# Two waits in GpSimd's scatter bursts of a routed expert kernel

## The reference

```python
x = x + _L0_attn_ref(_layernorm(x, axis=-1), ...)
x = x + _L0_ffn_ref(_layernorm(x, axis=-1), ...)
# within _L0_ffn_ref, N = 2048, TOP_K = 6, E = 64, C = 384:
topk_w, topk_idx = jax.lax.top_k(softmax(x @ gate_w.T), TOP_K)
pos = jnp.arange(A) - offsets[se]              # place of a token in its expert's list
buf = jnp.zeros((E, C, D)).at[se, pos_c].add(x[st])          # the scatter
eo = einsum(silu(einsum(buf, w_gate)) * einsum(buf, w_up), w_down)
y = jnp.zeros_like(x).at[st].add(eo[se, pos_c] * sw)
```

## Time and profile before

| what | us |
|---|---|
| median of 3 timed runs | 542.45 (541.57 to 545.41) |
| span of the profiled execution | 581.2 |
| start, 0 to 43 | 43.0 |
| attention and routing steps, 43 to 238.7 | 195.70 |
| tail of routing, 238.7 to 276.3 | 37.60 |
| loop over experts, 276.3 to 545 | 268.70 |
| closing, 545 to 581.2 | 36.2 |

### The profile page before, as it was taken

One profiled execution on the slowest core, in us unless ns is written; L12 is line 12 of the kernel. 1 busy time (PEld: TensorE's weight loads), 2 busy tenths in 40 slices (PEclk: granted clock), 3 DMA queues, 4 the chain that ended last, 5 costly groups with the idle time before them and its releaser, 6 DMA issues.

```text
span 581.2 us, 13626 instructions
## 1 busy us (share of the span) xinstructions
PE 528.9 (91%) x4267; PEld 446.2 (77%) x4267; DVE 348.5 (60%) x1107; ACT 301.3 (52%) x899; POOL 334.4 (58%) x365
## 2 busy tenths in 40 slices
PE   8799998988989894969999999999988999999991
PEld 7698988888889883858877878787766787778681
DVE  4968877777777874756554555555454555455512
ACT  3797777778777863311234444455544444445410
POOL 4482254555444546575146766766666676678840
PEclk9898998889777976899999999999999999999997
DMA  9999997722222222122999999999989999977556
GB/s 292 388 373 394 404 390 280 228 84 84 73 74 74 83 74 88 57 98 78 321 267 300 252 245 230 236 244 251 251 217 231 241 238 233 231 143 115 73 116 140
DMA packets 65857, 119.01 MB, mean 205 GB/s; under 512 B 11216, under 2 KB 43280, under 8 KB 62704
## 3 DMA queue, kind: packets, MB, share of 16 engines
q0 software_dynamic: 24576, 56.39, 37.0%
q1 hardware_dynamic: 39584, 58.75, 33.2%
q10 hardware_dynamic: 1616, 2.90, 1.4%
HBM read 57.28 MB, written 60.23 MB: 202 GB/s over the span
## 4 chain that ended last, share of the span: by engine, by line
PE 75%; DVE 7%; issue 4%; another core or an unknown queue 4%; ACT 4%; POOL 2%; DMA 1%; ACTq 0%; DVEq 0%
PE PS L958 17%; PE PS L976 9%; PE PS L962 7%; PE PS L979 7%; PE PS L629 4%; PE PS L945 4%; PE PS L696 4%; PE PS L809 3%; PE PS L767 3%; PE PS L609 3%; PE PS L784 2%; PE PS L713 2%; PE PS L795 2%; PE PS L719 2%
## 5 line engine op out<-in xcount | busy, mean ns | idle before, releaser
L1836 POOL DMA_INDIRECT expert_rows<-XR,slot x96 | 95.1, 990 | 86.9 <-PE PS L629 58.7
L1859 POOL DMA_INDIRECT out<-YE,dest x64 | 93.6, 1462 | 45.2 <-issue 24.7
L1859 POOL DMA_INDIRECT acc_b<-YE,dest x64 | 93.7, 1465 | 37.4 <-issue 14.0
L1234 ACT ACTIVATE YE<-PS,wsel 104x256 f32<-104x256 f32 (+14 forms) x128 | 53.4, 467 | 96.5 <-PE PS L979 78.1
L1061 ACT ACTIVATE SMX<-SMX,smax 128x112 f32<-128x112 f32 x256 | 75.0, 392 | 0.2 <-DVE smax L1464 0.2
L1649 DVE TENSOR_TENSOR HE<-SL,PS 128x216 f32<-128x216 f32 (+12 forms) x64 | 23.2, 362 | 52.0 <-ACT SL L1221 39.5
L1070 ACT COPY PT<-PS 112x512 f32<-112x512 f32 x64 | 36.0, 595 | 21.0 <-remote 15.8
L767 PE MATMUL PS<-VW,PT 112*64 112x17 f32 x960 | 35.8, 213 | 11.2 <-issue 11.2
L1640 DVE COPY XET<-PS 128x432 f32<-128x432 f32 (+12 forms) x64 | 36.5, 572 | 15.6 <-PE PS L945 11.4
L1626 DVE SCALAR_TENSOR_TENSOR hit<-XG,by_rank 112x12 f32<-112x12 f32 (+3 forms) x64 | 14.6, 229 | 49.3 <-DMA out<-YE,dest 33.7
L767 PEld LDWEIGHTS PS<-VW,PT 112*64 112x64 f32 x960 | 32.6, 140 | 14.8 <-issue 12.7
(11 more groups left out here) (236 smaller groups left out, 1146.0 us busy)
## 6 DMA issues: line engine op xcount, KB each, us to landing
expert_rows<-zero POOLq DMA_DIRECT2D x24, 1088.0 KB, 14.0
W<-in_w SPq DMA_DIRECT2D x24, 368.0 KB
XG<-expert_rows SPq DMA_DIRECT2D x24, 238.0 KB
XB<-in_w SPq DMA_DIRECT2D x15, 368.0 KB
SMX<-in_w SPq DMA_DIRECT2D x15, 368.0 KB
XG<-expert_rows SPq DMA_DIRECT2D x24, 204.0 KB
W<-in_w SPq DMA_DIRECT2D x24, 128.0 KB
XG<-expert_rows SPq DMA_DIRECT2D x10, 272.0 KB
```

Of the source, the lines that this page charges most:

```text
L1234: act.mul(YE[0:h, e.slot, t, :], PS[0:h, 5 + t, e.odd * D:(e.odd + 1) * D], wsel[0:h, e.slot, t:t + 1]).then_inc(y_ready, 1)
L1836: pool.indirect_dma_start(rows, bass.IndirectOffsetOnAxis(ap=slot[:, d2 % UN, k:k + 1], axis=0), XR[:, d2 % UN, :], None, bounds_check=EX ...
L1859: pool.indirect_dma_start(target, bass.IndirectOffsetOnAxis(ap=dest[0:h, e.slot, t:t + 1], axis=0), YE[0:h, e.slot, t, :], None, bounds_ch ...
```

## The change

Before block `d2`'s first scatter GpSimd waits until all six scatters of the block before have landed. Before the fourth it waits until the first three of the same block have landed (48 of the block's 96 counts). In block 13 this second wait stands ahead of the last block's rstd.

```diff
                     elif b1 >= NT:
 
                         pool.wait_ge(pv_done, RG * NT)
+                    if d2 > 0:
+
+                        pool.wait_ge(slot_stored[(d2 - 1) % UN], 96 * ((d2 - 1) // UN + 1))
                     for k in range(TOPK):
+                        if k == TOPK // 2:
+
+                            pool.wait_ge(slot_stored[d2 % UN], 96 * (d2 // UN) + 16 * k)
                         if c == NT - 1 and k == TOPK // 2:
                             root(c)
                         pool.indirect_dma_start(rows, bass.IndirectOffsetOnAxis(ap=slot[:, d2 % UN, k:k + 1], axis=0),
```

## The result

The changed kernel took **584.48 us** (median of 4 runs, 581.18 to 584.81) against 543.93 us (4 runs, 541.57 to 545.53) for the kernel before, timed beside it: ratio 1.0733, 95% interval 1.0686 to 1.0779. It is slower, as forecast, but by some 40 us and not by 10, far outside the range of 534 to 560.

The account below looks back on a forecast made before the run. TensorE's matmuls, broken by unexplained holes, were taken to bound the kernel before the experts; block 0 4.5, clock 1.4, ordinary blocks 1.0 and tail 3.1 made 10.0 us, added to 542.45 for 552.4 us, range 534 to 560 (8 in 10).

Parts of the forecast that it names:

- I take this step as the pattern: Ordinary blocks: one step of the profile, with 1.24 us of rstd cushion and 1.05 behind it, stands for all.
- everything ahead of the experts is later by the same 3.1: Tail: blocks 14 and 15 delay the last landing about as much as the last rstd, 3.1 us.
- Ordinary blocks, 1.0 us: Blocks 1 to 11: rstd 1.2 us later is mostly covered by its cushion; 0.1 us a block, 1 us in all.
- my upper bound of 1.4: Middle wait in an ordinary block: net price on GpSimd 1.2 us, range 0 to 1.4.
- met before it is reached in all steps: Wait at a block's start: already met in steps with 4 to 6 us of GpSimd idle time; matters only in the tail.
- The tail, 3.1 us: After the last scores: GpSimd sets the pace, and the last rstd comes 3.1 us later (1 to 5).
- Block 0, 4.5 us: Block 0's middle wait: scatters land behind queued zero-fill, so VectorE and TensorE stand still about 4.5 us (0 to 7).
- its clock, 1.4: Behind block 0's standstill: one TensorE step of scores at half clock, 1.4 us more (0 to 3).
- block 1 pays nothing more: Block 1: rstd ends near 100 and is wanted at 101.8 once steps are 4.5 later, so no added cost.
- The landing, 1.5 us: Middle wait: data land 1.5 us after a scatter's instruction ends, at most 1.71 by a row at routing's end.
- The first, TensorE's signals set free: Pauses in bursts release TensorE's held signals, winning 14 of 23.8 us; about 537 us (528 to 541); chance 0.24.
- The third, "the cushion is gone in every step": Unprofiled steps some 2 us shorter, so 11 blocks each pay 1.2 us: +13, 560 to 568 us; chance 0.06.

Follow-up runs that it names:

- the earlier trace: No change: the kernel before, in the single long profiled execution that the prediction read; its span is 581.2 us.
- before, again: No change: the kernel before, profiled a second time later; the profile spans 539.0 us, timed 541.81 us against 542.89.
- the run with blocks 2 to 10: Both waits added to the kernel before in blocks 2 to 10 only; 558.70 us against 543.14, ratio 1.0267.
- the run with blocks 11 to 15: Both waits added to the kernel before in blocks 11 to 15 only; 560.11 us against 543.14, ratio 1.0282.
- the run with blocks 0 and 1: Both waits added to the kernel before in blocks 0 and 1 only; 552.80 us against 541.76, ratio 1.0193.
- the run with the loose wait: Kernel before plus one wait per block: the second three scatters wait for all six of the block before; 543.94 us against 543.14, ratio 0.9979.
- The short pause: Kernel before plus 128x4 unused powers computed by GpSimd mid-burst in blocks 1 to 10, no landing wait; 548.41 us, ratio 1.0116.

## Why the prediction was wrong

Its sum was 4.5 + 1.4 + 1.0 + 3.1 = 10.0; the stretches give 9.1 + 14.4 + 17.3 = 40.8.

**Two steps failed.** The first is "I take this step as the pattern", by which the ordinary blocks were put at 1.0 us; they cost 14.4. The step of the earlier trace rows was of the long execution, 14.6 us where the step of before, again, is 11.03. It showed 4 to 6 us of idle time on GpSimd and 1.24 of cushion with 1.05 behind it; in before, again, there are 2.6 and 1.58, with nothing behind. In a step of 14.6 us GpSimd's new cycle of 11.75 fits, in one of 11.03 it doesn't. I had seen that the execution was 38.8 us over the median and had concluded that unprofiled steps must be shorter, and then kept the idle times of the long steps. A sum of costs can be carried over only if the cover is carried over as well, and here most of the cover was gone. The second is "everything ahead of the experts is later by the same 3.1", by which the tail was put at 3.1 us; it cost 17.3.

*Ordinary blocks, 1.0 us: measured 14.4* (15.6 by the run with blocks 2 to 10). Four things were wrong. The middle wait is 2.25 - 0.30 = 1.95 us net, above my upper bound of 1.4. The start wait, which I had "met before it is reached in all steps", now ends last in six of the eight ordinary steps, because the middle wait has pushed the burst's end toward the next one. GpSimd's own cycle of 11.75 us is over the step of 11.03, so no cushion of rstd can help: 8 x 0.72 = 5.8 us of the 14.4 are due whatever the order. And a landing has no fixed price: behind block 2 the start wait alone is 5.09 us.

*The tail, 3.1 us: measured 17.3* (17.0 by the run with blocks 11 to 15). The delays of blocks 12 and 13 that I worked out were small by the landing, but the larger error is the sentence "everything ahead of the experts is later by the same 3.1". The experts can't begin before the last landing, and ahead of that stand five steps of a chain that GpSimd bounds, each longer by 2.7 to 4.4 us. I priced the path to the last rstd instead of the one to the last scatter.

*Block 0, 4.5 us and its clock, 1.4: measured 9.1* (11.0 by the run with blocks 0 and 1). Here the mechanism was right and the size was off. The fourth scatter came 14.57 us after the first and not 13.0; 1.5 us later; and VectorE asked for rstd 90.86 - 8.03 - 72.02 = 10.8 us after the first scatter and not 12.7 (83.15 - 70.47 in the earlier trace rows), 1.9 us sooner. 4.5 + 1.5 + 1.9 = 7.9, against the 8.0 that VectorE waited. That block 1 pays nothing more was nearly right: its step is 13.9 us, 2.3 over before, again.

*The landing, 1.5 us.* At the end of routing the distance from the last scatter to SyncE's issue is the same 1.71 us as in the earlier trace rows (timelines of GpSimd and SyncE, changed kernel):

```profile
278.50 0.98 POOL L1842 DMA_INDIRECT expert_rows<-XR,slot  x1 [0.30 <-issue]
```

```profile
281.19 1.77 SPq L477 DMA_DIRECT2D XG<-expert_rows  x4
```

So the row was right, and it wasn't an upper bound for a wait on GpSimd itself, which takes 2.25. What makes the difference isn't shown. A likely part is that behind a wait GpSimd starts a scatter later than behind another scatter: 0.81 us after the unused powers, with no landing in it, against 0.30. 1.71 and the 0.5 between these make 2.2.

The Trainium skill, page "DMA: Bandwidth & Descriptors", section "Anatomy of one DMA — SWDGE (gpsimd) path", gave an estimated 2.3 us from the start of such a transfer. The trace is above it: from the start of the third scatter to the start of the fourth it is 0.97 + 2.25 = 3.22 us, of which the later start behind a wait may be 0.5.

*The clock.* It was put in once, behind block 0, at 1.4 us. The granted clock is low in all three stretches (0.85, 0.90 and 0.83), and TensorE's busy time grows by 2.3 us in the first and 6.6 in the middle one. Not all of this need be the change's: in the run with the loose wait, which loses nothing, TensorE is busy 89.5 us in these steps, 3.4 more than before, again, at a clock of 0.94. Nor did a gap decide it in the first profile: after a gap of 1.20 us TensorE's next scores took 3.05 us, after one of 1.24, one step earlier, 1.69.

*The rivals.* The first, TensorE's signals set free, was wrong: the holes were of that one execution, and a bound on scatters in flight by itself changes nothing (543.94 us). They did not belong to the profiling either, since before, again, was profiled as well. The third, "the cushion is gone in every step", with 0.06, came nearest. Its condition ("if unprofiled steps are some 2 us shorter") held, and stood in the prediction already, as the 38.8 us of excess. That its price of 13 us is close to the 14.4 is partly luck: it charged 1.2 us to each of 11 blocks for a lost cushion, while the cushion was 1.58 us, GpSimd's cycle makes 5.8 and two steps alone lose 6.4. It left out the tail, and with it another 14 us.

What the experiments leave open: how the 14.4 us of the ordinary blocks divide between rstd's lateness, GpSimd's cycle, the late landing behind block 2 and the clock, since of the two runs that moved rstd one put another wait in its place and the other fell between the bounds.

## What to carry to other kernels

A wait costs nothing only while the engine that waits has idle time that is longer than the wait, in a step of the usual length; before cushions are read from a profile, hold its span against the timed runs, and where it is 7% longer, take a second profile or shorten the idle times first. For an engine that issues transfers, add up its whole cycle with every wait in it and compare that with the step: once it was longer here, moving rstd forward won nothing. If transfers in flight are to be bounded, wait for those issued one group earlier: the same kind of bound was free here.

## What was not expected of the hardware

- A scatter behind the wait for the unused powers starts 0.81 us after their end, behind another scatter after 0.30 us.
- A scatter that waits for the three before it starts 10.87 us after the third's end where the queue is full of zero-fill, and about 2.3 us after it in ten other blocks.
- A stall of TensorE of 0.67 us was followed by about 3 us at a granted clock of 0.59, and the step behind it became 2 us longer; in the run with the loose wait the clock also fell in steps that have no idle time of TensorE over 0.23 us just ahead of it. The Trainium skill, page "TensorE: Matmul & The Clock Gate", section "HAM oscillation — how this bites in real kernels", has idle gaps as the cause. The short pause has a gap ahead of the fall, though one far shorter than the waits of that section's example; the steps of the loose wait show no such gap, and no run here shows the gap to be the cause.
